# Conditional linear attention on one core: the transposed x is loaded and normalised by GpSimd instead of being transposed by TensorE

## The reference, cut to what matters

```python
xn = _ln(x, ln_w, ln_b)                        # x: 128 sequences x 64 tokens x 256
q = xn @ Wq + bq
k = xn @ Wk + bk + (1.0 - src_mask) * -1000000.0
q = softmax(q.reshape(b, t, h, dh), axis=-1)   # 8 heads of 32
k = softmax(k.reshape(b, t, h, dh), axis=1)
v = ((xn @ Wv + bv) * src_mask).reshape(b, t, h, dh)
att = einsum('bnhd,bnhl->bhdl', k, v)
y = einsum('bnhd,bhdl->bnhl', q, att).reshape(b, t, d)
scale, shift = split(silu(emb) @ W_emb + b_emb, 2)
hh = _ln(y, ln2_w, ln2_b) * (1.0 + scale) + shift
return x + silu(hh) @ W_out + b_out
```

## Time and profile before

| what | before |
|---|---|
| median of 3 runs | 322.28 us (321.87 to 325.95) |
| the profiled execution | 323.25 us |
| its span in the profile | 321.4 us |
| granted TensorE clock, mean | 0.992 of full speed |
| busy: PE, PEld, DVE, ACT, POOL | 96%, 82%, 86%, 60%, 71% |

### The profile page before, as it was taken

How to read it: one execution, slowest core, us unless ns; L and a number is a source line. 1 busy time by engine, 2 the same in 40 slices (tenths; PEclk the granted TensorE clock), 3 DMA queues, 4 the chain that set the end, 5 groups by cost and what they waited for, 6 DMA issues and landing times.

```text
span 321.4 us, 14568 instructions
## 1 busy us (share of the span) xinstructions
PE 308.0 (96%) x5664; PEld 263.4 (82%) x5664; DVE 275.1 (86%) x749; ACT 193.0 (60%) x378; POOL 229.4 (71%) x276
## 2 busy tenths in 40 slices
PE   7899989999999999999999999999999999999974
PEld 6577867887988898988888898988889898988864
DVE  3775989889797998989898989989898989988883
ACT  1449384667486575668485675757575765756360
POOL 2170459778778687878887787878788887889550
PEclk9999999999999999999999999999999999999979
DMA  7930301050412204040403214050403110010023
GB/s 213 353 110 0 100 4 37 2 167 4 130 38 72 92 8 155 2 163 0 131 32 97 66 42 121 0 163 0 145 19 119 44 65 0 12 55 2 4 68 131
DMA packets 21706, 23.84 MB, mean 74 GB/s; under 512 B 1073, under 2 KB 19121, under 8 KB 21682
## 3 DMA queue, kind: packets, MB, share of 16 engines
q1 hardware_dynamic: 20192, 21.89, 22.0%
q10 hardware_dynamic: 1490, 1.62, 1.5%
HBM read 15.12 MB, written 8.39 MB: 73 GB/s over the span
## 4 chain that ended last, share of the span: by engine, by line
PE 82%; DVE 7%; DMA 4%; issue 2%; ACT 1%; POOL 1%; SPq 1%; POOLq 1%; DVEq 0%
PE bv L890 27%; PE bk L890 27%; PE by L890 13%; PE by L966 4%; PE by L945 4%; PE bv L957 4%; PE by L1026 4%; DMA x_all<-in_x 4%; DVE ystat L769 1%; DVE xstat L621 1%; DVE y_s L760 1%; DVE xt_lo L789 1%; DVE k_t L800 1%; ACT xhat L550 1%; POOLq L45 1%
## 5 line engine op out<-in xcount | busy, mean ns | idle before, releaser
L349 POOL TENSOR_TENSOR k_t<-k_t,kmax 128x512 f32<-128x512 f32 x32 | 34.4, 1074 | 26.3 <-DVE kmax L804 26.3
L496 ACT ACTIVATE k_t<-k_t 128x512 f32<-128x512 f32 x32 | 20.0, 626 | 44.5 <-POOL k_t L349 44.5
L267 POOL TENSOR_TENSOR z_s<-z_s,mod_shift 128x512 f32<-128x512 f32 x30 | 30.7, 1043 | 14.2 <-DVE z_s L720 14.2
L360 POOL TENSOR_TENSOR h_lo<-h_s,h_hi 128x512 fp32r<-128x512 f32 x30 | 38.5, 1306 | 2.9 <-ACT h_hi L513 2.3
L368 POOL TENSOR_TENSOR x_all<-x_all,bo_all 128x1024 f32 (+1 forms) x16 | 38.9, 2434 | 0.0
L550 ACT ACTIVATE xhat<-x_all,xr 128x256 f32 (+1 forms) x62 | 32.2, 591 | 4.6 <-DVE xr L632 3.1
L416 POOL TENSOR_SCALAR y_s<-y_s,yr 128x256 f32<-128x256 f32 x60 | 32.7, 558 | 2.5 <-POOL yr L413 2.2
L800 DVE SCALAR_TENSOR_TENSOR k_t<-off,bk 128x512 f32<-128x512 f32 x32 | 21.9, 683 | 14.5 <-PE bk L890 14.5
L890 PE MATMUL bv<-w_o_hi,h_hi 128*128 128x256 f32 x120 | 32.3, 288 | 0.0
L890 PE MATMUL bv<-w_o_lo,h_hi 128*128 128x256 f32 x120 | 32.2, 290 | 0.0
L520 ACT ACTIVATE xt_hi<-by 128x512 fp32r<-128x512 f32 x32 | 17.4, 597 | 23.4 <-PE by L1026 23.4
(11 more groups left out here) (128 smaller groups left out, 867.2 us busy)
## 6 DMA issues: line engine op xcount, KB each, us to landing
x_all<-in_x SPq DMA_DIRECT2D x15, 512.0 KB, 4.6
out<-x_all SPq DMA_DIRECT2D x15, 512.0 KB, 3.2
off<-in_mask_rows SPq DMA_DIRECT2D x16, 256.0 KB, 3.3
x_all<-in_x SPq DMA_DIRECT2D x2, 256.0 KB, 3.7
z_s<-in_w_emb ACTq DMA_DIRECT2D x1, 512.0 KB, 9.7
h_s<-in_w_emb ACTq DMA_DIRECT2D x1, 512.0 KB, 12.3
out<-x_all SPq DMA_DIRECT2D x2, 256.0 KB, 2.6
y_s<-in_wk ACTq DMA_DIRECT2D x1, 256.0 KB, 3.8
```

What stands on the lines that cost most here:

```text
L267: return eng.tensor_tensor(z, z, mod_shift[:, c, span(g, GB)].unsqueeze(2).broadcast_to([P, GB, SEQ]), ALU.add)
L349: nc.gpsimd.tensor_tensor(kk, kk, kmax[:, c, :].unsqueeze(2).broadcast_to([P, GB, SEQ]), ALU.subtract).then_inc(ksub_d, 1)
L360: nc.gpsimd.tensor_tensor(h_lo[:, c, :], h_s[:, c, :], h_hi[:, c, :].bitcast(fp32), ALU.subtract).then_inc(hlo_d, 1)
L496: nc.scalar.activation(k_t[:, parity, c, :], k_t[:, parity, c, :], ACT.Exp).then_inc(kexp_d, 1)
```

## The change

x is passed a second time, transposed (`x_t`). SP loads it group by group into `xt_raw`, channels on partitions. In that layout scale and offset differ along the row, so GpSimd's `xr` values (now rows 2 and 3 of `xr`) are stored to memory by SP as 1024 single numbers (`rows_stored`) and loaded again, repeated on all 128 partitions, as `rows` (`rows_loaded`, 512 KB written to SBUF). GpSimd multiplies and adds them in four instructions (`x_scaled`, two for each half of the channels). ScalarE rounds the result to `xt_hi` and VectorE forms `xt_lo`, now at the end of the turn before and from `xt_raw` in SBUF. Only group 0 is still made with `xhat` and transposes. The statistics of x are taken three groups ahead (flag S). The four normalising instructions of y go from GpSimd to ScalarE at the start of the following turn, except for group 14. GpSimd's `shifts` now come before both halves of `k_shifted`, and ScalarE and VectorE have a new order. The core of the diff:

```diff
-        xhat = sb("xhat", [P, 2, T, D])
+        xhat = sb("xhat", [P, T, D])
+        xt_raw = sb("xt_raw", [P, 2, C, GT])
+        rows = sb("rows", [P, 2, GT])
+        rows_dram = nc.dram_tensor("rows_dram", (2, 2, GT), fp32).ap()
...
-                body(i, i % 2, i + 1 < G, 0 <= i < G, 0 <= i - 1 < G, 0 <= i - 2 < G)
+                body(i, i % 2, i + 1 < G, 0 <= i < G, 0 <= i - 1 < G, 0 <= i - 2 < G, i + 3 < G)
...
+            def load_xt(g, parity):
+                sp.dma_start(xt_raw[:, parity, :, :], xt_h[:, :, span(g, GT)]).then_inc(xt_in[parity], 16)
+
+            def rows_stored(g, parity):
+
+                wait(sp, xr_d, 4 * g + 4)
+                wait(sp, rows_in, 16 * g - 32)
+                sp.dma_start(rows_dram[parity].rearrange("k (t p) -> p k t", p=P), xr[:, 2:4, :], allow_slow_non_contiguous=True
+                             ).then_inc(rows_out, 16)
+
+            def rows_loaded(g, parity):
+
+                wait(sp, rows_out, 16 * g)
+                wait(sp, xs_d, 2 * g - 2)
+                sp.dma_start(rows[:, :, :].rearrange("p k n -> p (k n)").unsqueeze(1),
+                             rows_dram[parity:parity + 1].rearrange("o k n -> o (k n)").unsqueeze(0)
+                             .broadcast_to([P, 1, 2 * GT])).then_inc(rows_in, 16)
...
+            def body(i, par, N, F, B, O, S):
+
+                if S:
+                    if not (isinstance(i, int) and i < 0):
+                        wait(sp, xstat_d, 4 * i + 5)
+                    load_x(i + 3, 1 - par)
                 if N and not (isinstance(i, int) and i < 1):
-                    wait(sp, xstat_d, 4 * i)
-                    load_x(i + 1, 1 - par)
                     wait(sp, kadd_d, 2 * i)
                     load_off(i + 1, 1 - par)
+                if not (isinstance(i, int) and i + 2 >= G):
+                    rows_stored(i + 2, par)
                 if O and not (isinstance(i, int) and i < 3):
                     store(i - 3)
+                if not (isinstance(i, int) and i + 2 >= G):
+                    if not (isinstance(i, int) and i < 0):
+                        if not first(i):
+                            wait(sp, lo_d, 2 * i + 2)
+                        load_xt(i + 2, par)
+                    rows_loaded(i + 2, par)
...
+            def x_scaled(g, parity, c):
+
+                if c == 0:
+                    wait(pool, rows_in, 16 * g)
+                    wait(pool, xt_in[parity], 8 * (g + parity))
+                xc = xt_raw[:, parity, c, :]
+                nc.gpsimd.tensor_tensor(xc, xc, rows[:, 0, :], ALU.mult).then_inc(xm_d, 1)
+                wait(pool, xm_d, 2 * g + c - 1)
+                nc.gpsimd.tensor_tensor(xc, xc, rows[:, 1, :], ALU.add).then_inc(xs_d, 1)
+
+            def x_rstd(g):
+
+                wait(pool, xhat_d, 4)
+                wait(pool, rows_out, 16 * g - 16)
+                wait_apart(pool, xmv_d, 4 * g + 4)
+                nc.gpsimd.tensor_scalar(xr[:, 0, :], xmv[:, :, 1], 1.0, EPS, ALU.mult, ALU.add).then_inc(xr_d, 1)
+                wait(pool, xr_d, 4 * g + 1)
+                nc.gpsimd.tensor_tensor(xr[:, 2, :], xr[:, 0, :], neg_half[:, :], ALU.pow).then_inc(xr_d, 1)
+                wait(pool, xr_d, 4 * g + 2)
+                nc.gpsimd.tensor_tensor(xr[:, 1, :], xmv[:, :, 0], xr[:, 2, :], ALU.mult).then_inc(xr_d, 1)
+                wait_apart(pool, xr_d, 4 * g + 3)
+                nc.gpsimd.tensor_scalar(xr[:, 3, :], xr[:, 1, :], -1.0, 1.0, ALU.mult, ALU.add).then_inc(xr_d, 1)
+
+            def y_scale(g):
+
+                wait(pool, yhat_d, 4 * g)
+                wait(pool, yve_d, 2 * g + 2)
+                nc.gpsimd.tensor_tensor(yr[:, 1, :], yr[:, 0, :], neg_half[:, :], ALU.pow).then_inc(yr_d, 1)
+                wait(pool, yr_d, 2 * g + 1)
+                nc.gpsimd.tensor_tensor(yr[:, 3, :], yr[:, 2, :], yr[:, 1, :], ALU.mult).then_inc(yr_d, 1)
...
+                    x_rstd(1)
+                    return
                 if O:
                     if isinstance(i, int) and i == 2:
                         pool.wait_ge(mod_ready, C)
                     shifts(i - 2)
+                k_shifted(i, par, 0)
+                k_shifted(i, par, 1)
+                if first(i):
+                    x_rstd(2)
                 if last_turn(i):
-                    k_shifted(i, par, 1)
                     x_biased(i)
...
+                for c in range(C):
+                    if O:
                         h_low(i - 2, c)
-                if F and not last_turn(i):
-                    k_shifted(i, par, 1)
+                    if N:
+                        x_scaled(i + 1, 1 - par, c)
                 if B:
-                    g = i - 1
-                    wait(pool, yhat_d, 4 * g)
-                    wait(pool, yve_d, 2 * g + 2)
-                    nc.gpsimd.tensor_tensor(yr[:, 1, :], yr[:, 0, :], neg_half[:, :], ALU.pow).then_inc(yr_d, 1)
-                    wait(pool, yr_d, 2 * g + 1)
-                    nc.gpsimd.tensor_tensor(yr[:, 3, :], yr[:, 2, :], yr[:, 1, :], ALU.mult).then_inc(yr_d, 1)
-                    wait_apart(pool, yr_d, 2 * g + 2)
+                    y_scale(i - 1)
...
+                if last_turn(i):
+                    pool.wait_ge(yr_d, 2 * M + 2)
                     for t in range(T):
                         nc.gpsimd.tensor_scalar(y_s[:, t, :], y_s[:, t, :], yr[:, 1, t:t + 1], yr[:, 3, t:t + 1],
                                                 ALU.mult, ALU.add).then_inc(yhat_d, 1)
-                if F and not last_turn(i):
+                if S:
+                    x_rstd(i + 3)
+                if not last_turn(i):
                     x_biased(i)
...
+            def x_high(g, parity, c):
+
+                wait(act, xs_d, 2 * g + c - 1)
+                wait(act, qv_d, 4 * g)
+                nc.scalar.activation(xt_hi[:, c, :], xt_raw[:, parity, c, :], ACT.Copy).then_inc(hi_d, 1)
+
+            def y_hat_all(g):
+
+                wait(act, yr_d, 2 * g + 2)
+                for t in range(T):
+                    nc.scalar.activation(y_s[:, t, :], y_s[:, t, :], ACT.Identity, scale=yr[:, 1, t:t + 1],
+                                         bias=yr[:, 3, t:t + 1]).then_inc(yhat_d, 1)
...
+                if O:
+                    y_hat_all(i - 2)
...
                 if B:
-                    exp_k_copied(i - 1)
-                    q_exp(i - 1, 1 - par)
-                if F:
-                    k_exp(i, par, 0)
-                if B:
+                    exp_k_copied(i - 1, 0)
+                    q_exp(i - 1, 1 - par, 1)
+                    exp_k_copied(i - 1, 1)
                     q_copied(i - 1)
                 if O:
                     z_tanh(i - 2)
-                if F:
-                    if isinstance(i, int) and i == 0:
-                        weights_qv_high()
-                        act.wait_ge(emb_done, 1)
-                        for j in range(2 * C):
-                            nc.scalar.activation(emb[:, j, :], be[1][:, j * BATCH:(j + 1) * BATCH], ACT.Identity,
-                                                 scale=0.5, bias=b_e[:, j:j + 1]).then_inc(emb_out, 1)
-                    v_tile(i, par, 0)
-                    v_tile(i, par, 1)
+                    h_high(i - 2, 0)
+                if first(i):
+                    weights_qv_high()
+                    act.wait_ge(emb_done, 1)
+                    for j in range(2 * C):
+                        nc.scalar.activation(emb[:, j, :], be[1][:, j * BATCH:(j + 1) * BATCH], ACT.Identity,
+                                             scale=0.5, bias=b_e[:, j:j + 1]).then_inc(emb_out, 1)
+                v_tile(i, par, 0)
+                v_tile(i, par, 1)
                 if O:
+                    h_high(i - 2, 1)
+                k_exp(i, par, 0)
+                k_exp(i, par, 1)
+                if N:
+                    mask_offset(i + 1, 1 - par)
+                v_tile(i, par, 2)
+                v_tile(i, par, 3)
+                q_exp(i, par, 0)
+                if N:
                     for c in range(C):
-                        h_high(i - 2, c)
-                if N:
-                    g = i + 1
-                    wait(act, xr_d, 4 * g + 4)
-                    wait(act, xt_d, 2 * g - 2)
-                    for t in range(T) if not (isinstance(g, int) and g == 0) else (0, 1):
-                        nc.scalar.activation(xhat[:, 1 - par, t, :],
-                                             group_of(x_all, g)[:, :, t * D:t * D + D].rearrange("p g n -> p (g n)"),
-                                             ACT.Identity, scale=xr[:, 1, t:t + 1],
-                                             bias=xr[:, 3, t:t + 1]).then_inc(xhat_d, 1)
-                if F:
-                    if last_turn(i):
-                        k_exp(i, par, 1)
-                    v_tile(i, par, 2)
-                    v_tile(i, par, 3)
-                    if not last_turn(i):
-                        k_exp(i, par, 1)
```

(75 more changed lines are left out.)

142 lines of the change are left out of this document (64 added, 78 removed).

## The result

The changed kernel takes 454.62 us (449.32 to 456.75, 4 runs) against 323.0 us for the kernel before in the runs beside it: 1.394 times (95% interval 1.376 to 1.413), far outside my range. Two of the four, 456.75 and 456.58 us, count as slow, and the ratio is that of the other two, 449.32 and 452.67 us. The profiled execution is the fastest of the four, 449.32 us.

What follows compares the result with a forecast made beforehand. GpSimd, with its blocks, was to replace TensorE as the bound at 19.3 us a turn. Span 321.4 + 11.8 (loop) - 0.9 (end) + 1.0 (start) = 333.3, giving 334 us as the likeliest time; range 318 to 344.

Steps and rivals of the forecast that it cites:

- I put it between 2 and 10 us, hidden in the loop in both cases: Landing time of the store of 1024 single numbers, with about 15 us available for it in each turn.
- Rival (c): Trip through memory over 13 to 15 us makes GpSimd wait for rows each turn; at 20 us, 395 us; chance 0.04.
- 1 MB more a turn leaves room: In the loop's DMAs, the added loads fit beside today's 74 GB/s.
- The blocks: VectorE and GpSimd SBUF instructions hold each other up: three blocks of 0.45 to 0.55 us, 1.6 a GpSimd turn.
- x_scaled: 1.22 taken: GpSimd's four scaling instructions cost 1.22 us each, 5.0 in all with a small gap; bounds 4.2 to 5.1.
- rival (a): TensorE stays the bound: x_scaled costs 1.04, blocks fall on tiny instructions; turn 17.0, 311 us; chance 0.13.
- TensorE 17.0, GpSimd 19.3 a turn: Loop turn: TensorE loses 0.87 us of transposes; GpSimd needs 17.7 plus 1.6 of blocks and sets the turn.
- the loop over K and z: Path from x_scaled through K to z_scaled: z ready at some 18.8 us, GpSimd free at 19.4, so hardly idle.
- The start: Before the loop: K of group 1 starts 1.9 us later, less 0.87 for group 2's transposes: +1.0 us.
- The turns 2 to 14: Turn 2 unchanged, ten turns of 19.3 and two of 17.2 us: 227.4 against 215.6, +11.8.
- the end: Turn 15 has no x_scaled and GpSimd does y's tiles as before: -0.87 us.
- The sign: Whole kernel: slower with chance 0.61, same 0.26, faster 0.13; likeliest 3.7% slower.

Runs made afterwards that it cites:

- e1: Changed kernel with scale and offset stored as one contiguous 32-byte piece per partition instead of 1024 pieces of 4 bytes; 345.39 us, 1.067 times the kernel before.
- e2: Kernel before plus, in turns 1 to 14, a store of a constant 128x8 tile in 1024 adjacent 4-byte pieces; 404.92 us, 1.249 times.
- e4: Kernel before plus, in turns 1 to 14, the change's two 512 KB loads into unused tiles, without the store; 328.91 us, 1.014 times.
- e8: e1 with b_out added to only one column of each tile of x, 2.2 us less GpSimd work a turn; 342.62 us, 1.059 times the kernel before.
- e6: Kernel before plus the 1024 pieces of 4 bytes, landing in SBUF instead of memory; 324.08 us, 1.0028 times.
- e7: Kernel before plus 1024 pieces of 4 bytes read from adjacent places of memory instead of written; 323.12 us, 1.0005 times.
- e15: Kernel before plus the store of 1024 pieces of 4 bytes, each number 16 bytes from the next; 323.69 us, 0.9989 times.
- e5: Kernel before plus the store of 1024 pieces of 4 bytes, each number 512 bytes from the next; 322.62 us, 1.0007 times.
- e13: Kernel before plus the 1024-piece store ordered by partition, each partition writing its 8 numbers into 32 bytes of its own; 362.76 us, 1.124 times.
- e9: Kernel before plus the adjacent 4-byte store from 127 instead of 128 partitions, 1016 pieces; 350.48 us, 1.085 times.
- e3: Kernel before plus, in turns 1 to 14, a store of a constant 128x4 tile in 512 adjacent 4-byte pieces; 384.64 us, 1.183 times.
- e11: e2 with its store issued some 6 us later in each turn, behind the first maximum of q; 371.65 us, 1.148 times the kernel before.

## Why the prediction was wrong

**The failed step: "I put it between 2 and 10 us, hidden in the loop in both cases".** Both halves failed. The store lands after 9.2 us at the start, but after 10.4 to 13.4 in the loop; and with "hidden" the sum went wrong, in which the store has no term in the loop. I asked only who waits for the numbers, and there nobody does: rows has its 15 us. I did not ask who else stands still while they are written: TensorE, and the loads. That is worth 109 us in the changed kernel (454.62 against e1's 345.39) and 80 in the kernel before (e2). Rival (c) had the trip through memory as its place, but with the wrong mechanism, GpSimd waiting for rows: that wait comes once in the changed kernel, at the start, with 4.6 us. The Trainium skill (Runtime: NRT & Kernel Launch, Instruction fetch mechanics) says that each engine's instructions are refilled in blocks through a DMA queue. That made me think of missing instructions for the 64.3 us of "issue", but the trace doesn't bear it out: of e2's 24 instruction packets on the page (17 in q8, 7 in q14) none lies between 120 and 366 us, where most of the holes are.

**"1 MB more a turn leaves room": nearly.** e4 prices it at 4 us, 1.4% [0.8, 2.0].

**The blocks: right in size, not in place.** In e1 h_s has a mean of 1152 ns instead of the 640 of the earlier trace rows, and its two instances of one turn show 1.36 and 1.17 where 0.70 is the free length; x_scaled's first instruction of that turn takes 1.76 and the unhindered ones 1.30. Three blocks of 0.45 to 0.55 fall into that turn, as forecast, but on k_shifted, x_scaled's first instruction and yr, not on k_shifted, h_low and x_scaled's last. Two groups of e1's page, part 5:

```profile
L413 POOL TENSOR_TENSOR xt_raw<-xt_raw,rows 128x512 f32<-128x512 f32 x30 | 43.6, 1454 | 0.6 <-DMA rows<-rows_dram 0.6
L844 DVE SCALAR_TENSOR_TENSOR h_s<-th,z_s 128x512 f32<-128x512 f32 x30 | 34.3, 1152 | 0.0
```

**x_scaled: 1.22 taken, 1.25 to 1.30 measured** where nothing hinders it, at the upper end of my bounds (5.1 for four, 1.28 each) and a little over it; rival (a)'s 1.04 never occurs.

**TensorE 17.0, GpSimd 19.3 a turn.** e1's steady turn is 18.7 to 18.9, half a us under the forecast: GpSimd is busy for 18.1 to 18.2, not for 19.3. That next behind it stands the loop over K and z at 18.8 after GpSimd's 19.4 was right in kind: e8 finds it 0.5 us below.

**What puts e1 at a span of 343.4 instead of my 333.3.** Three terms. The start: turn 2's y transposes begin at 55.84 instead of 49.08, +6.8 where I had +1.0. The chain of e1 shows why: the statistics of group 2 wait for their load, which I had only placed in VectorE's schedule and not in the DMA's.

```profile
21.44 5.61 DMA x_all<-in_x
27.05 0.02 issue
27.07 1.40 DVE xstat L694 x4
```

The turns 2 to 14 take 14.1 us more than before, where I had 11.8: the steady ones are shorter than forecast, but one takes 22.1 us, with a hole of 3.25 in TensorE's products (up to 270.53) that no run explains, and the end adds 1.1 instead of taking away 0.9. Together 5.8 + 2.3 + 2.0 = 10.1.

**The sign** was right, 0.61 on slower; e1 at 345 lies just over my 344. The size that was measured was covered by no rival.

**What stays open** is what makes adjacent 4-byte writes slow in the chip. Shown: only writes into memory (e6, e7), only at a distance under 16 bytes (e15), with the same packets and a later landing (e2, e5), less when a partition's own numbers are the neighbours (e13) and less with 127 partitions (e9). The Trainium skill (DMA: Bandwidth & Descriptors, Specifications) states that writes under 512 bytes read, modify and write; were that the whole, e5 and e15 would pay as well, and they don't. It is also open what TensorE lacks in the holes. Missing instructions are argued, not shown: the trace shows an engine that waits for no semaphore and stands still some us behind the store, in both kernels and not without it, but no instruction packet then. A rival that no run tests is the profiler: every time here comes with a span and a granted clock, so it was taken with the profiler on, and its records thin out with the holes (of the steps of the added store's semaphore e2's trace has 113, e5's 224). If what stalls TensorE is the writing of its own records, the loss would be smaller without it.

## What to carry to other kernels

A DMA has a price for those who don't wait for it: when a change adds one of an unusual form, bound not only its landing time but what it does to loads, and to TensorE with its many short instructions, whose first sign is idle time put down to "issue". Small numbers that must go through memory did no harm in one piece of 32 bytes for each partition, in rows of 512 bytes, or 16 bytes and more from one to the next. And a relief of 0.87 us on the engine that leads is worth nothing when the work goes to one that, with its blocks, then needs 1 us more than the first did.

## What the runs showed of the hardware

- 1024 writes of 4 bytes to adjacent places of memory, one DMA: 9.2 us to land at the start and 10.4 to 13.4 in the loop of the changed kernel, and 5.7 us lost a turn in a kernel that doesn't wait for it (e2); 512 of them 4.3 us (e3). At 16, 32, 64 or 512 bytes apart, into SBUF, or as reads: the medians stay within 0.5% of the kernel before, and the landing takes 3.2 to 4.2 us in the median.
- The pieces themselves leave as fast in the slow case as in the harmless one (the last 2.4 to 3.8 us after the issue in e2 and e5). The DMA engines may show no packet at all (share 0.00 from 177 to 184 in e2) while TensorE still does nothing.
- Loads issued right behind such a store land late: 13.7 to 15.1 us instead of 3.4 to 5.1 for 512 KB of x (e11).
- After a hole of 3.4 to 4.8 us TensorE's clock is granted at 0.50 (the 1.2 GHz level), and the same tiles take 1.05 instead of 0.63 us, which makes each hole dearer than its length.
- With the store later in the turn (e11) VectorE and ScalarE wait up to 6.8 us in front of tiles that TensorE fills. Many of TensorE's semaphore steps come 0.9 to 5.1 us behind the modelled ends of its instructions there, in the kernel before none by more than 0.1.
